# A 64-step recurrence: z stored into the accumulating PSUM bank by identity products

## Chip, cores and metric

The kernel runs on one core of one Trainium2 chip. The metric is the device time of one execution in microseconds, the median of several runs. All data are fp32.

## What is computed

The reference is an audio tower of four layers over 64 sequences of 246 tokens and 128 features. The change touches one stage of it, the recurrence inside the third layer's attention ("L2_attn", 8 heads of 64 features). In the form in which the kernel computes it, for every token position, head and step t of 64:

```
e_t    = exp(h_{t-1} - max h_{t-1});  r_t = 1 / sum(e_t)        (64 features)
w_s    = r_t * (K_s . e_t)                       for the n = t + 1 steps s <= t
h_t    = z_t + sum over s <= t of w_s * U_s      (64 features, stored as result hs)
```

e_0 is all ones and r_0 is 1/64. K, U and z (`kr`, `ur`, `zz`) come from the stage before. So the work of a step grows with t, and h_t is needed before step t + 1 of the same chain can start.

## The kernel before

`recur_stage` (from L2494) holds the whole recurrence. Two dynamic loops run over 4 pairs of heads and 2 halves of the token positions: 8 passes. Within a pass 123 positions are cut into two groups `a` of 62 and 61 positions; with 2 heads each, a group fills 124 or 122 partitions. All 64 steps are written out by hand, and the two groups alternate, so that one works on VectorE while the other is on TensorE. K, U, z of a pass are loaded in 4 chunks of 16 steps on SP's queue (`s_in`), and `Hh` holds z and is overwritten step by step with h.

For one group and one step (n = t + 1), in the order of the dependences:

- VectorE, `dots`: K times e into `pr` (L2608, n x 64 elements), reciprocal of the sum (L2610), sum over features into `dot` (L2613), scale and parity mask into `w` (L2615, `s_dot`).
- TensorE turns w (L2587): a transpose of 124 partitions by 2n columns into `wT` (`s_tr`).
- ScalarE, `spread` (L2563): copies wT into the block-diagonal weights `W` (`s_dg`).
- TensorE (L2596): 62 or 61 products, one a position, of 2n rows by 32 columns with 64 moving columns, four at a time in four column groups, added up in one PSUM bank `acc[a]` (`s_sum`). A product for one position contributes zeros to the other rows of its 32, which is why 16 of them share a column group.
- VectorE, `finish`: adds z, h = acc + z into `Hh` (L2621), then the negated maximum (L2622, `s_mx`).
- ScalarE, `exped` (L2569): e = exp(h + mx) with the sum as accumulator output, which shows as a second row, ACTIVATION_READ_ACCUMULATOR (`s_ex`).

Each engine takes its instructions in program order. VectorE: dots(0,t), finish(1,t-1), dots(1,t), finish(0,t). ScalarE: spread(0,t), exped(1,t-1), spread(1,t), exped(0,t). TensorE: turn(0,t), products(0,t), turn(1,t), products(1,t). SP stores a chunk of `Hh` once both groups' maxima of its last step are done (L2552 to L2555).

Of the kernel before, what the change touches and what calls it, by code (L numbers as in the profile page):

```python
# [8 lines left out]
ALU = mybir.AluOpType  # L9
# [432 lines left out]
SC = 8  # L442
# [1688 lines left out]
FD = 64  # L2131
# [362 lines left out]
def recur_stage(nc, c, kr, ur, zz, hs):  # L2494
# [8 lines left out]
    with Stage(nc, "recur") as st:  # L2503
# [10 lines left out]
        rs = [st.sb(f"rs{a}", [CP, 1]) for a in range(2)]  # L2514
        ri = [st.sb(f"ri{a}", [CP, 1]) for a in range(2)]
        wT = [st.ps(f"wT{a}", [128, 512]) for a in range(2)]
        acc = [st.ps(f"acc{a}", [128, 512]) for a in range(2)]
        s_in = [st.sem(f"loaded{k}") for k in range(NL)]
        s_own = [st.sem(f"own{a}") for a in range(2)]
        s_dot = [st.sem(f"dots{a}") for a in range(2)]  # L2520
# [2 lines left out]
        s_sum = [st.sem(f"summed{a}") for a in range(2)]  # L2523
        s_mx = [st.sem(f"max{a}") for a in range(2)]
        s_ex = [st.sem(f"exp{a}") for a in range(2)]
        s_out = st.sem("stored")
        V = nc.vector

# [8 lines left out]
        with nc.Fori(0, FH // 2) as i, nc.Fori(0, 2) as half, st.step() as block:  # L2537
            @block.sync
            def _(sp):
                chains = lambda t, a: t[i, bass.ds(half * HT + GROUPS[a][0], GROUPS[a][1])].rearrange("t h s d -> (t h) s d")  # L2540
                for k in range(NL):
                    r = slice(k * SC, (k + 1) * SC)
                    for a, (t0, tg) in enumerate(GROUPS):
                        for p in (slice(0, 112), slice(112, 2 * tg)):
                            sp.dma_start(K[a][p, r, :], chains(kr, a)[p, r, :]).then_inc(s_in[k], 16)
                            sp.dma_start(Hh[a][p, r, :], chains(zz, a)[p, r, :]).then_inc(s_in[k], 16)
                        sp.dma_start(U[a][2 * SC * k:2 * SC * (k + 1), 0:tg, :],
                                     ur[i].rearrange("s h t d -> (s h) t d")[2 * SC * k:2 * SC * (k + 1), bass.ds(half * HT + t0, tg), :]).then_inc(s_in[k], 16)
                for k in range(NL):
                    r = slice(k * SC, (k + 1) * SC)  # L2550
                    for a, (t0, tg) in enumerate(GROUPS):
                        sp.wait_ge(s_mx[a], (k + 1) * SC)  # L2552
                        for p in (slice(0, 112), slice(112, 2 * tg)):
                            sp.dma_start(hs[i].rearrange("s t h d -> (t h) s d")[bass.ds(half * (2 * HT) + 2 * t0 + p.start, p.stop - p.start), r, :],
                                         Hh[a][p, r, :]).then_inc(s_out, 16)  # L2555
                sp.wait_ge(s_out, 64 * NL)

            @block.scalar
            def _(act):
                def spread(a, t):  # L2560
                    n, tg = t + 1, GROUPS[a][1]
                    act.wait_ge(s_tr[a], n)
                    nc.scalar.activation(W[a][0:2 * n, 0:34 * TG].rearrange("p (m x) -> p m x", x=34)[:, 0:tg, 0:2],  # L2563
                                         wT[a][0:2 * n, 0:2 * tg].rearrange("p (m h) -> p m h", h=2), ACT.Copy).then_inc(s_dg[a], 1)

                def exped(a, t):
                    cp = 2 * GROUPS[a][1]
                    act.wait_ge(s_mx[a], t + 1)
                    nc.scalar.activation(e[a][0:cp], Hh[a][0:cp, t, :], ACT.Exp, bias=mx[a][0:cp, 0:1],  # L2569
                                         accum_out=rs[a][0:cp, 0:1]).then_inc(s_ex[a], 1)  # L2570

                for t in range(SL):
                    spread(0, t)
                    if t:
                        exped(1, t - 1)
                    spread(1, t)
                    if t + 1 < SL:
                        exped(0, t)

            @block.tensor  # L2580
            def _(pe):
                for t in range(SL):
                    n = t + 1
                    for a, (t0, tg) in enumerate(GROUPS):
                        cp = 2 * tg
                        pe.wait_ge(s_dot[a], n)
                        nc.tensor.transpose(wT[a][0:2 * n, 0:cp], w[a][0:cp, 0:n, :].rearrange("p s h -> p (s h)"),  # L2587
                                            c.ident[0:cp, 0:cp]).then_inc(s_tr[a], 1)
                        if t % SC == 0:
                            pe.wait_ge(s_in[t // SC], 160)  # L2590
                        pe.wait_ge(s_dg[a], n)
                        for j in range(16):
                            for q in range(4):
                                m = 16 * q + j
                                if m < tg:
                                    ins = nc.tensor.matmul(acc[a][32 * q:32 * q + 32, 0:FD], W[a][0:2 * n, WQ * q + 32 * j:WQ * q + 32 * j + 32],  # L2596
                                                           U[a][0:2 * n, m, :], start=(j == 0), stop=(j == 15 or m + 1 == tg))
                        ins.then_inc(s_sum[a], 1)

            @block.vector  # L2600
            def _(dve):
# [16 lines left out]
                def finish(a, t):  # L2618
                    cp = 2 * GROUPS[a][1]
                    dve.wait_ge(s_sum[a], t + 1)  # L2620
                    own[a](V.tensor_tensor(Hh[a][0:cp, t, :], acc[a][0:cp, 0:FD], Hh[a][0:cp, t, :], ALU.add))  # L2621
                    V.tensor_reduce(mx[a][0:cp], Hh[a][0:cp, t, :], AX.X, ALU.max, negate=True).then_inc(s_mx[a], 1)  # L2622

                for a in range(2):
                    own[a](V.memset(e[a][:], 1.0))
# [1129 lines left out]
```

## Time and profile before

| | us |
|---|---|
| median of 3 runs | 25499.4 |
| lowest, highest | 25471.2, 25502.3 |
| profiled execution | 25494.0 |
| its span | 25492.3 |
| of the span, recurrence (8 passes) | about 13960 to 21110 |

Over the whole span TensorE's products are busy 15738.5 us (62%), VectorE 12959.8 (51%), ScalarE 5715.3 (22%), GpSimd 2368.2 (9%). A line of the span in 40 slices shows where each engine works, as a digit for tenths of its time; the recurrence is slices 22 to 33:

```profile
PE   3423577745457787787787665565466554455776
DVE  6512455551153343343343777877877782213555
ACT  0001244411023333333333100000010001123442
PEclk9566566657679999999998555555555556676776
```

PE is TensorE's products and PEld its weight loads, which overlap them; DVE is VectorE, ACT ScalarE. PEclk is the clock that TensorE was granted, in tenths of 2.4 GHz.

### The profile page before, as it was taken

What the parts mean: (1) busy time and instruction counts of PE and PEld (TensorE: products, weight loads), DVE (VectorE), ACT (ScalarE), POOL (GpSimd) and SP (SyncE); (2) the same over time, 40 slices, a digit from 0 to 9 for tenths busy, and PEclk for the clock granted to TensorE, in tenths of its full rate; (3) what the DMA queues carried; (4) which work ended last, traced back from release to release, by engine and by line L of the source; (5) the groups of instructions that cost most, each with busy time, mean ns of one, the idle gap of its engine ahead of it and who ended that gap; (6) DMA issues with size and microseconds to landing.
All of it is one profiled execution on the core that took longest, in us unless ns stands there. A gap on an engine that the chain in (4) does not pass through costs nothing. (4 is left out here: it accounts for less than half of the span.)

```text
span 25492.3 us, 660904 instructions
## 1 busy us (share of the span) xinstructions
PE 15738.5 (62%) x292639; PEld 13161.1 (52%) x292639; DVE 12959.8 (51%) x23794; ACT 5715.3 (22%) x12048; POOL 2368.2 (9%) x1280
## 2 busy tenths in 40 slices
PE   3423577745457787787787665565466554455776
PEld 2412566633246666666666554555455444344554
DVE  6512455551153343343343777877877782213555
ACT  0001244411023333333333100000010001123442
POOL 0063000013501011011010000000000000010001
PEclk9566566657679999999998555555555556676776
DMA  0222100022221101101101011011101104004663
GB/s 17 80 38 59 36 14 14 14 62 60 36 61 17 18 17 17 18 17 17 18 17 29 14 26 24 7 26 26 22 12 26 25 6 139 19 20 146 187 182 89
DMA packets 1549770, 1066.76 MB, mean 42 GB/s; under 512 B 819722, under 2 KB 1473965, under 8 KB 1528109
## 3 DMA queue, kind: packets, MB, share of 16 engines
q1 hardware_dynamic: 1319715, 967.03, 15.3%
q0 software_dynamic: 227328, 57.19, 1.5%
q8 instruction: 2466, 40.40, 0.7%
q14 instruction: 261, 2.14, 0.0%
HBM read 537.19 MB, written 484.53 MB: 40 GB/s over the span
## 5 line engine op out<-in xcount | busy, mean ns | idle before, releaser
L2596 PE MATMUL recur_acc<-recur_U,recur_W 2*32 2x64 f32 (+7 forms) x125952 | 3713.9, 311 | 552.9 <-ACT recur_W L2563 385.1
L2596 PEld LDWEIGHTS recur_acc<-recur_U,recur_W 2*32 2x32 f32 (+7 forms) x125952 | 3467.5, 172 | 850.7 <-ACT recur_W L2563 629.3
L2608 DVE TENSOR_TENSOR recur_pr<-recur_K,recur_e 124x64 f32<-124x64 f32 (+60 forms) x1024 | 2381.1, 2325 | 817.7 <-ACT recur_e L2569 694.9
L2276 PE MATMUL delta_pS<-delta_B 64*64 64x64 f32 x55104 | 2287.4, 234 | 792.4 <-issue 783.5
L2276 PEld LDWEIGHTS delta_pS<-delta_B 64*64 64x64 f32 x55104 | 2035.2, 145 | 1338.1 <-issue 1333.5
L2395 DVE TENSOR_TENSOR delta_U<-delta_U,delta_pR 128x256 f32<-128x256 f32 x1968 | 828.6, 421 | 3386.8 <-PE delta_pR L2276 3379.4
L2613 DVE TENSOR_REDUCE recur_dot<-recur_pr 124x1 f32<-124x64 f32 (+60 forms) x1024 | 2375.8, 2320 | 35.4
L2350 ACT ACTIVATE delta_B<-delta_pS 128x512 f32<-128x512 f32 (+1 forms) x1968 | 1067.7, 543 | 4449.7 <-PE delta_pS L2276 4449.7
L2587 PE MATMUL recur_wT<-const_ident,recur_w 124*2 124x124 f32 (+60 forms) x1024 | 424.5, 415 | 2457.6 <-DVE recur_w L2615 2455.6
L2276 PE MATMUL delta_pR<-delta_U,delta_B 64*64 64x64 f32 x39360 | 1725.6, 224 | 303.0 <-DVE delta_Z L2404 192.4
L2563 ACT ACTIVATE recur_W<-recur_wT 2x124 f32<-2x124 f32 (+60 forms) x1024 | 287.1, 280 | 6504.2 <-PE recur_wT L2587 6504.2
L2276 PEld LDWEIGHTS delta_pR<-delta_U,delta_B 64*64 64x64 f32 x39360 | 1510.9, 140 | 333.2 <-issue 206.1
L2587 PEld LDWEIGHTS recur_wT<-const_ident,recur_w 124*2 124x2 f32 (+60 forms) x1024 | 133.4, 130 | 2677.7 <-DVE recur_w L2615 2634.1
L2381 POOL TENSOR_TENSOR delta_QK<-delta_QK,delta_mx 128x1536 f32<-128x1536 f32 x123 | 339.4, 2760 | 5306.1 <-DVE delta_mx L2409 5306.1
L2276 PE MATMUL delta_gp<-delta_W,delta_xc 128*128 128x16 f32 x1476 | 767.9, 603 | 33.5 <-DVE delta_xc L2389 33.5
L2276 PE MATMUL delta_pR<-delta_P,delta_B 64*64 64x64 f32 x15744 | 674.8, 221 | 90.6 <-DVE delta_P L2401 73.1
L1206 PE MATMUL experts_tp<-const_ident,experts_xg 123*128 123x123 f32 x256 | 49.5, 328 | 1093.8 <-DMA experts_xg<-xp,experts_ij 1093.8
L2823 POOL IOTA choice_ios<- 123x64 f32 x1 | 0.2, 185 | 7715.6 <-POOLq L78 7715.6
L2276 PEld LDWEIGHTS delta_pR<-delta_P,delta_B 64*64 64x64 f32 x15744 | 585.9, 134 | 145.9 <-issue 117.4
L1167 POOL DMA_INDIRECT hB<-experts_y,experts_ij x256 | 616.5, 2408 | 370.8 <-DVE experts_y L1185 200.2
L2276 PE MATMUL delta_gp<-delta_KT 64*64 64x64 f32 x11808 | 531.7, 223 | 159.9 <-ACT delta_KT L2369 98.4
L1206 PEld LDWEIGHTS experts_tp<-const_ident,experts_xg 123*128 123x128 f32 x256 | 37.1, 172 | 1122.4 <-DMA experts_xg<-xp,experts_ij 1104.9
(574 smaller groups left out, 27572.6 us busy)
## 6 DMA issues: line engine op xcount, KB each, us to landing
scr<-rel_BD SPq DMA_DIRECT2D x128, 1288.0 KB
rel_sc<-scr SPq DMA_DIRECT2D x128, 861.0 KB
xnT<-ln_xT SPq DMA_DIRECT2D x64, 492.0 KB, 3.0
kr<-delta_QK SPq DMA_DIRECT2D x492, 64.0 KB
ur<-delta_Uf SPq DMA_DIRECT2D x492, 64.0 KB
zz<-delta_Z SPq DMA_DIRECT2D x492, 64.0 KB
recur_K<-kr SPq DMA_DIRECT2D x64, 448.0 KB
recur_H<-zz SPq DMA_DIRECT2D x64, 448.0 KB
```

What stands on the lines that cost most here:

```text
L1167: nc.gpsimd.indirect_dma_start(acc[:, :], bass.IndirectOffsetOnAxis(ap=ij[:, k, t:t + 1], axis=0), y[:, k, t, :], None, compute_op=ALU.add ...
L1206: nc.tensor.transpose(tp[:, t, 0:HT], xg[:, k, t, 0:D], c.ident[0:HT, 0:HT]).then_inc(s_tp, 1)
L2276: return nc.tensor.matmul(o, l, r, start=True, stop=True)
L2350: nc.scalar.activation(later(k, l + 1)[0][:, :, 0:m, :], pS[k][:, :, 0:m, :], ACT.Copy).then_inc(s_ac[k], 1)
L2381: nc.gpsimd.tensor_tensor(qk, qk, wide_of(mx), ALU.subtract).then_inc(s_sh, 1)
L2395: V.tensor_tensor(later(k, l + 1)[1][:], u[:], pR[k][l % 2][:, 0:4, :], ALU.subtract if l == 0 else ALU.add).then_inc(s_dv[k], 1)
L2563: nc.scalar.activation(W[a][0:2 * n, 0:34 * TG].rearrange("p (m x) -> p m x", x=34)[:, 0:tg, 0:2], wT[a][0:2 * n, 0:2 * tg].rearrange("p ( ...
L2587: nc.tensor.transpose(wT[a][0:2 * n, 0:cp], w[a][0:cp, 0:n, :].rearrange("p s h -> p (s h)"), c.ident[0:cp, 0:cp]).then_inc(s_tr[a], 1)
L2596: ins = nc.tensor.matmul(acc[a][32 * q:32 * q + 32, 0:FD], W[a][0:2 * n, WQ * q + 32 * j:WQ * q + 32 * j + 32], U[a][0:2 * n, m, :], start ...
L2608: V.tensor_tensor(pr[a][0:cp, 0:n, :], K[a][0:cp, 0:n, :], e[a][0:cp, None, :].to_broadcast([cp, n, FD]), ALU.mult).then_inc(s_own[a], 1)
L2613: own[a](V.tensor_reduce(dot[a][0:cp, 0:n], pr[a][0:cp, 0:n, :], AX.X, ALU.add))
L2823: nc.gpsimd.iota(ios[:], pattern=[[1, CS]], base=0, channel_multiplier=0, allow_small_or_imprecise_dtypes=True).then_inc(s_po, 1)
```

## The change

z_t is no longer added by VectorE. Ahead of a step's turn TensorE multiplies z_t, as it lies in `Hh`, by the four 32-column slices of the identity matrix (`start=True`), so the PSUM bank begins with z_t, and all the other products add to it (`start=False`). The maximum and the exponential read the bank in PSUM. ScalarE copies the bank into `Hh` behind the exponential (`keep`, a new semaphore `s_cp`). Each group has two banks, used by even and odd steps; the identity products of step t wait for the copy of step t - 2. SP's stores wait for the copy where they waited for the maximum. TensorE's wait for the loads moves ahead of the turn.

```diff
-        acc = [st.ps(f"acc{a}", [128, 512]) for a in range(2)]
+        acc = [[st.ps(f"acc{a}{q}", [128, 512]) for q in range(2)] for a in range(2)]
...
+        s_cp = [st.sem(f"kept{a}") for a in range(2)]
...
-                        sp.wait_ge(s_mx[a], (k + 1) * SC)
+                        sp.wait_ge(s_cp[a], (k + 1) * SC)
...
-                    nc.scalar.activation(e[a][0:cp], Hh[a][0:cp, t, :], ACT.Exp, bias=mx[a][0:cp, 0:1],
+                    nc.scalar.activation(e[a][0:cp], acc[a][t % 2][0:cp, 0:FD], ACT.Exp, bias=mx[a][0:cp, 0:1],
                                          accum_out=rs[a][0:cp, 0:1]).then_inc(s_ex[a], 1)
+
+                def keep(a, t):
+                    cp = 2 * GROUPS[a][1]
+                    act.wait_ge(s_mx[a], t + 1)
+                    nc.scalar.activation(Hh[a][0:cp, t, :], acc[a][t % 2][0:cp, 0:FD], ACT.Copy).then_inc(s_cp[a], 1)
 
                 for t in range(SL):
                     spread(0, t)
                     if t:
                         exped(1, t - 1)
+                        keep(1, t - 1)
                     spread(1, t)
                     if t + 1 < SL:
                         exped(0, t)
+                    keep(0, t)
+                keep(1, SL - 1)
...
+                        if t % SC == 0:
+                            pe.wait_ge(s_in[t // SC], 160)
+                        if t >= 2:
+                            pe.wait_ge(s_cp[a], t - 1)
+                        for q in range(4):
+                            nc.tensor.matmul(acc[a][t % 2][32 * q:32 * q + 32, 0:FD], c.ident[0:cp, 32 * q:32 * q + 32], Hh[a][0:cp, t, :],
+                                             start=True, stop=False)
                         pe.wait_ge(s_dot[a], n)
                         nc.tensor.transpose(wT[a][0:2 * n, 0:cp], w[a][0:cp, 0:n, :].rearrange("p s h -> p (s h)"),
                                             c.ident[0:cp, 0:cp]).then_inc(s_tr[a], 1)
-                        if t % SC == 0:
-                            pe.wait_ge(s_in[t // SC], 160)
                         pe.wait_ge(s_dg[a], n)
                         for j in range(16):
                             for q in range(4):
                                 m = 16 * q + j
                                 if m < tg:
-                                    ins = nc.tensor.matmul(acc[a][32 * q:32 * q + 32, 0:FD], W[a][0:2 * n, WQ * q + 32 * j:WQ * q + 32 * j + 32],
-                                                           U[a][0:2 * n, m, :], start=(j == 0), stop=(j == 15 or m + 1 == tg))
+                                    ins = nc.tensor.matmul(acc[a][t % 2][32 * q:32 * q + 32, 0:FD], W[a][0:2 * n, WQ * q + 32 * j:WQ * q + 32 * j + 32],
+                                                           U[a][0:2 * n, m, :], start=False, stop=(j == 15 or m + 1 == tg))
...
-                    own[a](V.tensor_tensor(Hh[a][0:cp, t, :], acc[a][0:cp, 0:FD], Hh[a][0:cp, t, :], ALU.add))
-                    V.tensor_reduce(mx[a][0:cp], Hh[a][0:cp, t, :], AX.X, ALU.max, negate=True).then_inc(s_mx[a], 1)
+                    V.tensor_reduce(mx[a][0:cp], acc[a][t % 2][0:cp, 0:FD], AX.X, ALU.max, negate=True).then_inc(s_mx[a], 1)
```

## Rows read from the trace of the kernel before

**Rows 1.** The page's groups: count, busy us, mean ns, idle before

```profile
L2596 PE MATMUL recur_acc<-recur_U,recur_W 2*32 2x64 f32 (+7 forms) x125952 | 3713.9, 311 | 552.9 <-ACT recur_W L2563 385.1
L2608 DVE TENSOR_TENSOR recur_pr<-recur_K,recur_e 124x64 f32<-124x64 f32 (+60 forms) x1024 | 2381.1, 2325 | 817.7 <-ACT recur_e L2569 694.9
```

**Rows 2.** Windows (length, PE, PEld, DVE, ACT, POOL busy, clock, DMA), and one burst

```profile
14060.00:14150.00 90.00, 82.33 (x2601) 72.77 (x2597) 50.97 (x123) 14.01 (x63) 0.00 (x0) 0.50 0.02 4
...
14700.00:14850.00 150.00, 60.84 (x1859) 53.11 (x1853) 136.49 (x91) 8.99 (x45) 0.00 (x0) 0.61 0.01 2
...
14652.44 3.33 PE L2596 MATMUL recur_acc<-recur_U,recur_W 108*32 108x64 f32 x124 [0.38 <-ACT recur_W L2563]
```

**Rows 3.** Timeline (start, us, engine, line) of a half-step at n = 10

```profile
14104.70 0.09 PEld L2587 LDWEIGHTS recur_wT<-const_ident,recur_w 122*20 122x20 f32 x1 [0.17 <-issue]
14104.71 0.37 PE L2587 MATMUL recur_wT<-const_ident,recur_w 122*20 122x122 f32 x1
...
14105.09 0.22 DVE L2622 TENSOR_REDUCE recur_mx<-recur_H 124x1 f32<-124x64 f32 x1
14105.12 0.28 ACT L2563 ACTIVATE recur_W<-recur_wT 20x122 f32<-20x122 f32 x1 [3.64 <-PE recur_wT L2587]
14105.35 0.35 ACT L2569 ACTIVATE recur_e<-recur_H,recur_mx 124x64 f32<-124x64 f32 x1
...
14105.45 3.63 PE L2596 MATMUL recur_acc<-recur_U,recur_W 20*32 20x64 f32 x122 [0.36 <-ACT recur_W L2563]
```

**Rows 4.** Timeline of TensorE: turns that end n = 3, 16, 21, and the next

```profile
14044.55 0.37 PE L2587 MATMUL recur_wT<-const_ident,recur_w 122*6 122x122 f32 x1
...
14156.39 0.39 PE L2587 MATMUL recur_wT<-const_ident,recur_w 122*32 122x122 f32 x1
...
14200.93 0.39 PE L2587 MATMUL recur_wT<-const_ident,recur_w 122*42 122x122 f32 x1 [0.24 <-DVE recur_w L2615]
...
14205.69 0.40 PE L2587 MATMUL recur_wT<-const_ident,recur_w 124*44 124x124 f32 x1 [0.38 <-DVE recur_w L2615]
```

**Rows 5.** Timeline of a half-step at n = 62

```profile
14806.54 0.35 DVE L2615 SCALAR_TENSOR_TENSOR recur_w<-recur_dot,recur_ri,recur_par 124x124 f32<-124x124 f32 x1
14806.81 0.22 DVE L2621 TENSOR_TENSOR recur_H<-recur_acc,recur_H 122x64 f32<-122x64 f32 x1
...
14806.94 0.47 PE L2587 MATMUL recur_wT<-const_ident,recur_w 124*124 124x124 f32 x1 [5.78 <-DVE recur_w L2615]
14807.06 0.22 DVE L2622 TENSOR_REDUCE recur_mx<-recur_H 122x1 f32<-122x64 f32 x1
14807.45 0.29 ACT L2563 ACTIVATE recur_W<-recur_wT 124x124 f32<-124x124 f32 x1 [9.66 <-PE recur_wT L2587]
14807.62 0.34 ACT L2569 ACTIVATE recur_e<-recur_H,recur_mx 122x64 f32<-122x64 f32 x1
...
14808.08 4.29 DVE L2608 TENSOR_TENSOR recur_pr<-recur_K,recur_e 122x3968 f32<-122x3968 f32 x1 [0.80 <-ACT recur_e L2569]
```

**Rows 6.** Timeline of weight loads, last stage, then the stage behind the recurrence

```profile
25303.31 0.49 PEld L3654 LDWEIGHTS last_p<-last_ws,last_xa 128*123 128x123 f32 x2 [0.23 <-issue]
25304.03 0.48 PEld L3653 LDWEIGHTS last_p<-last_be,last_hx 16*123 16x123 f32 x2 [0.23 <-issue]
...
21140.88 0.95 PEld L2708 LDWEIGHTS dout_yp<-dout_wo,dout_tT 128*123 128x123 f32 x8
21141.75 0.46 PEld L2699 LDWEIGHTS dout_tp<-const_ident,dout_t 123*128 123x128 f32 x4
```

**Rows 7.** ScalarE's groups by form: count, busy us, mean ns, idle before

```profile
L2569 ACT ACTIVATE recur_e<-recur_H,recur_mx 124x64 f32<-124x64 f32 x504 | 171.1, 340 | 0.0
L1483 ACT ACTIVATE liquid_a<-liquid_pp,liquid_cols 128x64 f32<-128x64 f32 x246 | 77.2, 314 | 227.8 <-PE liquid_pp L1475 227.8
...
L2362 ACT ACTIVATE delta_sb<-delta_sb 128x16 f32<-128x16 f32 x123 | 26.5, 216 | 1.4
L2357 ACT ACTIVATE delta_sb<-delta_gp 128x16 f32<-128x16 f32 x123 | 22.5, 183 | 1.4
```

## The prediction

> **What bounds the kernel now.** I read the groups of instructions of the recurrence first, then its windows, then the timeline of one half-step from each part. A half-step is one group `a` at one step `t`; n = t + 1 is the number of stored steps that the dot products run over. There are 64 steps, 2 groups and 8 passes of the outer loops, so 1024 half-steps, 128 a pass. The busiest two groups [rows 1] are the products into `acc` on TensorE (L2596: 125952 rows for 1024 half-steps, 123 each, so a group's 62 or 61 fp32 products show as 124 or 122 rows) and the multiply of K by e on VectorE (L2608), whose mean hides that it grows with n.
>
> The windows [rows 2] show two parts. At 14060 to 14150 us TensorE is busy 82.33 us of 90 and VectorE 50.97: TensorE bounds it. At 14700 to 14850 VectorE is busy 136.49 us of 150 and TensorE 60.84: VectorE, or a chain through it, bounds it. ScalarE is busy 14.01 and 8.99 us, so it is never the bound by itself.
>
> In the first part a half-step is a ring on TensorE alone [rows 3]: the turn of w (L2587) starts at 14104.71, ScalarE spreads it at 14105.12, the products run 3.63 us from 14105.45, and the next turn follows. VectorE's maximum (14105.09) and the exponential (14105.35) lie under the products. From the last turn of n = 3 (14044.55) to the last of n = 16 (14156.39) are 26 half-steps [rows 4], 4.30 us each; to the last of n = 21 (14200.93) are 10 more, 44.54 us, already partly set by VectorE; the next takes 4.76.
>
> In the second part [rows 5] the ring is: w ready on VectorE (starts 14806.54), turn 14806.94, spread 14807.45, exponential of the *other* group 14807.62, VectorE's next multiply 14808.08. VectorE does the add (14806.81) and the maximum (14807.06 to 14807.28) beside the turn. The reader is to see what the exponential waits for: the maximum is done 0.34 us before it starts, while the spread started 0.17 us before it, and L2563 stands ahead of L2569 in ScalarE's queue. The add is not on this ring.
>
> **The add that goes.** It lasts 0.22 us and holds the maximum back by 0.25 (14806.81 to 14807.06) [rows 5]. In the second part nothing is gained: the maximum would be ready 0.59 us instead of 0.34 before an exponential that still queues behind the spread. VectorE just idles longer before L2608. In the first part the products are the cover: the exponential could move from 0.23 to 0.17 us behind the spread [rows 3, 5], under a burst of 3.63. So: 0. If that cover were gone it would be worth 0.25 a half-step (a rival below). The maximum reads PSUM instead of SBUF; the add read PSUM in the same 0.22 us, so I take no change, and it has 0.34 us of slack.
>
> **The exponential reads PSUM.** From SBUF with a bias column it takes 340 ns at 64 elements; the activation of another stage, 64 elements from PSUM with a bias column, takes 314; two 16-element ones take 216 from SBUF and 183 from PSUM [rows 7]. So 26 to 33 ns less, if it reaches the ring. I take 25 ns, bounds 0 and 35. It counts where the exponential is on the ring: n = 22 to 64, 43 x 2 x 8 = 688 half-steps: -17 us (bounds 0 and -24).
>
> **The identity products.** Four a half-step, fp32, 124 rows by 32 columns, so 8 more matmul rows. By the burst's own rate (3.63 us / 124 = 29.3 ns) [rows 3] they take 0.234 us. They stand before the turn in TensorE's queue. Where TensorE idles before the turn (5.78 us at n = 62 [rows 5]) they are free. Where it does not, all of it is on the ring, and so is a second thing: TensorE's pipeline empties when the size of tile changes. The turn's weight load in the first part starts after 0.17 us in which the loader waits for nothing shown [rows 3]; in the last stage, where 16-row and 128-row products alternate, it is 0.23 [rows 6]; where transposes and products of the same size alternate (L2699, L2708) there is none [rows 6]. The Trainium skill, TensorEngine Tiling (Array Packing), Key Properties, says that changing the tiling mode drains TensorE; these rows agree.
>
> For n up to 16 the burst has up to 32 rows, the identity products 124 by 32, the turn 124 by 2n, up to 32 columns. The emptying moves ahead of the identity products, and none is added behind them if the turn's tile is as small as its columns. Cost 0.24; lower bound 0.12 (one of two rounds of four hidden in the switch), upper 0.234 + 0.17 = 0.40. For n = 17 to 32 the turn has 34 to 64 columns, another size, so the emptying comes twice; I take 0.37, near the upper bound, since part of the 0.17 overlaps.
>
> Sum per pass: n = 4 to 16, 26 x 0.24 = 6.24. For n = 1 to 3, 6 x 0.24 = 1.44. For n = 17 to 21, ten half-steps of 4.31 + 0.37 = 4.68 are 46.8 in place of 44.54 [rows 4]: 2.26. From n = 22 the half-step (4.76) is longer than that and covers it. Together 9.94, x 8 = 79.5 us. With both lower bounds (0.12; 0.234 over n = 17 to 21, where only the shorter of the half-steps grow, about 1.1): 4.9 x 8 = 39. With 0.40 everywhere: (12.8 + 2.6) x 8 = 123.
>
> **Added waits.** TensorE waits on `s_cp` of step t - 2, with the turn and the products queued behind it: that copy was done a whole step earlier. Its wait on the loads moves ahead of the turn, but the turn needed dot products of the same loads. ScalarE's copy `keep` (about 0.28 us like L2563 [rows 3]) follows its exponential directly, and the next spread behind it comes over 3 us later. SP's stores wait for the copy in place of the maximum: at the end of a pass 0.25 goes and about 0.28 comes, 0. Two banks a group mean no reader is waited for.
>
> **The sum.** The profiled execution took 25494.0 us (span 25492.3), 5.4 below the median of 25499.4. 25494.0 + 79.5 - 17.2 = 25556. Bounds of the unknown costs together: 25494 + 39 - 24 = 25509 and 25494 + 123 = 25617. About 0.2% (51 us) is what a measurement of this kernel can tell from no change.
>
> **Rivals.**
> A, the forecast: 25556, chance 0.64.
> B, faster: the add does sit on the second part's ring, because the exponential's start is set by the maximum and not by the spread. For: the wait before L2608 is put down to the exponential, which needs the maximum. Against: the 0.34 us of slack [rows 5]. It decides if the exponential starts less than 0.17 us behind the spread once the maximum is early. Then 688 x 0.25 = 172 us go: 25384. Chance 0.08.
> C, nothing to be seen: the identity products slip into the time in which TensorE changes tile size, and the exponential gives its full 35 ns: 25490 to 25515. Against: a burst's products follow each other at 29.3 ns a row with no slack between them, so eight more rows should take their share. Chance 0.09.
> D, dearer: the turn is always of full width, so the emptying is paid twice at every n: 0.13 more on 32 half-steps x 8 = 33 us: 25589. For: the turn shows one row where an fp32 product shows two, so it runs in a mode of its own. Against: nothing in the trace separates it. Chance 0.16.
> The Trainium skill, the same page, Gotcha 2, says that column tiling excludes the transpose mode with fp32, which is rival D; no row here shows it.
> E, the clock: TensorE's granted clock is 0.50 (1.2 GHz) through the first part although it is busy 92% [rows 2], and 0.61 on average in the second, where the products have over 100 rows. If 124-row products lifted it in the first part, bursts would shorten: one that lay partly at 2.4 GHz took 3.33 us against 3.63 [rows 2, 3]. At 0.5 us for a whole burst, 32 x 8 x 0.5 = 128 us go: 25428. Against: 8 of 132 rows are few. Chance 0.03.
> The Trainium skill, TensorE: Matmul & The Clock Gate, Part 1, says that activity releases a clock that is halved by default; the 92% at 0.50 speaks against reading that by busy time alone.
>
> **How the numbers follow.** The forecast is the likeliest case's, 25556. Its own spread (25509 to 25617) straddles 25499 + 51 = 25550: of A's 0.64 I give 0.36 to slower and 0.28 to the same; D is slower (0.16), C the same (0.09), B and E faster (0.11). That is faster 0.11, same 0.37, slower 0.52. The range 25490 to 25617 leaves out B, E and a little of the rest.
>
> **What would show it.** Turn to turn at n = 4 to 16: 4.54 us, two-fold emptying 4.67, hidden 4.3. At n = 17 to 21: 4.68. At n = 62: 10.26 less 0.025, B 10.0. The exponential still 0.17 us behind the spread and the idle time before L2608 up from 0.80 to about 1.0. The exponential at 310 ns. What would make it wrong: another order on ScalarE's ring than I read, or the read of PSUM by two engines slowing one of them.

## Result and profile after

The changed kernel takes 25566.69 us in the median of 8 runs (25541.24 to 25592.09), the kernel before 25485.58 in 8 runs beside it (25471.23 to 25502.32). The ratio is 1.0031, with a 95% interval of 1.0020 to 1.0042: slower by about 0.3%. The forecast was 25556, and the time lies in its range (25490 to 25617). The profiled execution took 25571.98 us, 77.9 more than that of before.

The table counts from turn to turn of w on TensorE, all 8 passes added up, after less before; each number is a sum over the turns' starts in the two traces. A half-step counts to the step whose turn ends it.

| stretch | half-steps a pass | one before | one after | all, us | forecast, us |
|---|---|---|---|---|---|
| n = 1 to 3 | 6 | loads decide | | +6.1 | +11.5 |
| n = 4 to 16 | 26 | 4.30 | 4.67 | +77.5 | +49.9 |
| n = 17 to 21 | 10 | 4.31 to 4.64 | 4.69 to 4.70 | +19.3 | +18.1 |
| n = 22 to 64 | 86 | 10.26 at n = 62 | 10.23 | -23.9 | -17.2 |
| sum | 128 | | | +79.0 | +62.3 |

Between the passes and ahead of the first turn another -0.7 comes, which makes +78.3 at the last turn: the whole difference lies in the recurrence.

The half-step at n = 10 of after, which answers to [rows 3]. The view is the timeline: start, us, engine, line, operation, and in brackets the idle time before with what ended it.

```profile
14105.68 0.20 PEld L2600 LDWEIGHTS recur_acc<-recur_H,const_ident 122*32 122x32 f32 x8 [0.17 <-issue]
14105.68 0.44 PE L2600 MATMUL recur_acc<-recur_H,const_ident 122*32 122x64 f32 x8
...
14106.05 0.09 PEld L2603 LDWEIGHTS recur_wT<-const_ident,recur_w 122*20 122x20 f32 x1 [0.17 <-issue]
14106.05 0.38 PE L2603 MATMUL recur_wT<-const_ident,recur_w 122*20 122x122 f32 x1
14106.46 0.28 ACT L2564 ACTIVATE recur_W<-recur_wT 20x122 f32<-20x122 f32 x1 [4.01 <-PE recur_wT L2603]
14106.63 0.29 ACT L2570 ACTIVATE recur_e<-recur_acc,recur_mx 124x64 f32<-124x64 f32 x1
14106.79 3.39 PEld L2610 LDWEIGHTS recur_acc<-recur_U,recur_W 20*32 20x32 f32 x122 [0.65 <-ACT recur_W L2564]
14106.79 3.63 PE L2610 MATMUL recur_acc<-recur_U,recur_W 20*32 20x64 f32 x122 [0.36 <-ACT recur_W L2564]
...
14110.35 0.20 PEld L2600 LDWEIGHTS recur_acc<-recur_H,const_ident 124*32 124x32 f32 x8 [0.17 <-issue]
...
14110.72 0.38 PE L2603 MATMUL recur_wT<-const_ident,recur_w 124*22 124x124 f32 x1
```

The ring reads off the starts. Identity products to turn: 14105.68 to 14106.05, 0.37. Turn to burst: 0.74, as before [rows 3]. Burst to the next identity products: 3.56, just what it was from burst to turn (4.30 - 0.74). So the whole growth is the 0.37 between the start of the identity products and the turn, and in it stands the second 0.17 in which the weight loader waits for nothing shown. Before, there was one such gap; now there is one ahead of L2600 and one ahead of L2603.

The half-step at n = 62 of after, which answers to [rows 5], again from the timeline:

```profile
14811.97 0.35 DVE L2629 SCALAR_TENSOR_TENSOR recur_w<-recur_dot,recur_ri,recur_par 124x124 f32<-124x124 f32 x1
14812.23 0.22 DVE L2635 TENSOR_REDUCE recur_mx<-recur_acc 122x1 f32<-122x64 f32 x1
...
14812.87 0.29 ACT L2564 ACTIVATE recur_W<-recur_wT 124x124 f32<-124x124 f32 x1 [9.55 <-PE recur_wT L2603]
14813.04 0.31 ACT L2570 ACTIVATE recur_e<-recur_acc,recur_mx 122x64 f32<-122x64 f32 x1
...
14813.47 4.29 DVE L2622 TENSOR_TENSOR recur_pr<-recur_K,recur_e 122x3968 f32<-122x3968 f32 x1 [1.02 <-ACT recur_e L2570]
```

The add is gone and the maximum starts 0.25 us sooner, but the exponential still starts 0.17 behind the spread. The maximum is done at 14812.45, 0.59 before the exponential. VectorE's idle time before the next multiply is 1.02 instead of 0.80: what the add gave back is waited away, less the 0.03 by which the exponential is shorter.

Four groups of after over the recurrence (count, busy us, mean ns, idle before and what ended it), beside [rows 1]:

```profile
L2622 DVE TENSOR_TENSOR recur_pr<-recur_K,recur_e 124x64 f32<-124x64 f32 (+60 forms) x1024 | 2380.8, 2325 | 1133.4 <-ACT recur_e L2570 1008.1 <-DMA recur_U<-ur 125.3
L2600 PE MATMUL recur_acc<-recur_H,const_ident 124*32 124x64 f32 (+1 forms) x8192 | 532.7, 309 | 224.1 <-DMA recur_U<-ur 224.1
L2570 ACT ACTIVATE recur_e<-recur_acc,recur_mx 124x64 f32<-124x64 f32 x1008 | 301.4, 299 | 0.0
L2576 ACT ACTIVATE recur_H<-recur_acc 124x64 f32<-124x64 f32 (+1 forms) x1024 | 215.8, 211 | 30.6 <-DVE recur_mx L2635 30.6
```

VectorE waits 1133.4 us before its multiply instead of 817.7; the identity products are 8192 rows, 8 a half-step; the exponential takes 299 ns on average.

### The profile page after: what moved, and what is told of

Read it like the earlier page. It is cut to its first block and busy times, and to the rows that moved or that the text cites. A ratio compares the mean times of both kernels' runs of the same rounds, so it can differ in the third digit from the quotient of the medians.

```text
span 25570.0 us, 677290 instructions
## 1 busy us (share of the span) xinstructions
PE 16032.1 (63%) x300831; PEld 13367.6 (52%) x300831; DVE 12724.3 (50%) x22770; ACT 5774.8 (23%) x13072; POOL 2371.8 (9%) x1280
## 5 line engine op out<-in xcount | busy, mean ns | idle before, releaser
L2622 DVE TENSOR_TENSOR recur_pr<-recur_K,recur_e 124x64 f32<-124x64 f32 (+60 forms) x1024 | 2380.8, 2325 | 1133.4 <-ACT recur_e L2570 1008.1
L2603 PE MATMUL recur_wT<-const_ident,recur_w 124*2 124x124 f32 (+60 forms) x1024 | 424.5, 415 | 2034.6 <-DVE recur_w L2629 2033.0
L2603 PEld LDWEIGHTS recur_wT<-const_ident,recur_w 124*2 124x2 f32 (+60 forms) x1024 | 133.6, 130 | 2251.0 <-DVE recur_w L2629 2197.8
L2600 PE MATMUL recur_acc<-recur_H,const_ident 124*32 124x64 f32 (+1 forms) x8192 | 532.7, 309 | 224.1 <-DMA recur_U<-ur 224.1
```

Source lines behind the costliest of these rows:

```text
L2600: nc.tensor.matmul(acc[a][t % 2][32 * q:32 * q + 32, 0:FD], c.ident[0:cp, 32 * q:32 * q + 32], Hh[a][0:cp, t, :], start=True, stop=False)
L2622: V.tensor_tensor(pr[a][0:cp, 0:n, :], K[a][0:cp, 0:n, :], e[a][0:cp, None, :].to_broadcast([cp, n, FD]), ALU.mult).then_inc(s_own[a], 1)
```

## First set of experiments: which part costs, which gives

The theory is that of the prediction with one term grown: identity products ahead of the turn cost their time and a second emptying at every n up to 21; the add is worth nothing; the exponential's read of PSUM gives 0.035 a half-step from n = 22. The rival is that other parts carry the difference: the waits added on TensorE, the copy on ScalarE, or PSUM being read by two engines. All four kernels of this set are compared with the same runs of before, median 25509.9 us.

**Products alone.** The kernel before, with four products of K's rows by the identity slices into a bank that nobody reads.

```diff
+        spare = [st.ps(f"spare{a}", [128, 512]) for a in range(2)]
...
+                        if t % SC == 0:
+                            pe.wait_ge(s_in[t // SC], 160)
+                        for q in range(4):
+                            nc.tensor.matmul(spare[a][32 * q:32 * q + 32, 0:FD], c.ident[0:cp, 32 * q:32 * q + 32], K[a][0:cp, t, :],
+                                             start=True, stop=True)
                         pe.wait_ge(s_dot[a], n)
...
-                        if t % SC == 0:
-                            pe.wait_ge(s_in[t // SC], 160)
                         pe.wait_ge(s_dg[a], n)
```

> The kernel before, with four fp32 identity products (of K's rows, 124 by 32, 64 moving columns) added ahead of each turn into a spare PSUM bank that nobody reads. Nothing else of the change. Theory (the products and a second emptying of TensorE lie on TensorE's ring up to n = 21 and nowhere else): turn to turn 4.67 us at n = 4 to 16 against 4.30, 4.69 at n = 17 to 21, and exactly the old 10.26 at n = 62, so about +97 us over n = 4 to 21 and +100 in all, 20 to 25 us more than the whole change costs. Rival (the loss comes from two engines reading the accumulating bank, or from ScalarE's copy): this kernel costs under 20 us.

Measured 25616.76 us, ratio 1.0044 (1.0028 to 1.0059). Turn to turn at n = 4 to 16 it is 4.67, +77.5 us in all; n = 17 to 21 gives +19.2, n = 1 to 3 +5.3, n = 22 to 64 -0.1. These are after's own losses, with no add removed, no new wait on a copy, and no read moved. TensorE's wait for the loads stands ahead of the turn here too, as in the change. The timeline of this kernel at n = 8 has both gaps:

```profile
14108.76 0.20 PEld L2590 LDWEIGHTS recur_spare<-recur_K,const_ident 122*32 122x32 f32 x8 [0.17 <-issue]
...
14109.13 0.09 PEld L2593 LDWEIGHTS recur_wT<-const_ident,recur_w 122*16 122x16 f32 x1 [0.17 <-issue]
```

**No add.** The kernel before without the add of z; the maximum reads the bank in PSUM.

```diff
-                    own[a](V.tensor_tensor(Hh[a][0:cp, t, :], acc[a][0:cp, 0:FD], Hh[a][0:cp, t, :], ALU.add))
-                    V.tensor_reduce(mx[a][0:cp], Hh[a][0:cp, t, :], AX.X, ALU.max, negate=True).then_inc(s_mx[a], 1)
+                    V.tensor_reduce(mx[a][0:cp], acc[a][0:cp, 0:FD], AX.X, ALU.max, negate=True).then_inc(s_mx[a], 1)
```

> The kernel before with VectorE's add of z left out and the maximum taken from PSUM, so the result lacks z. Theory (the exponential waits behind the spread in ScalarE's queue, not for the maximum): turn to turn unchanged within 0.01 us at n = 62 and at n = 10, VectorE's idle time before its multiply up by 0.2 to 0.25, total within 10 us of before. Rival B (the add lies on the second part's ring): 0.25 us less a half-step from n = 22 on, 172 us less in all.

Measured 25502.61 us, ratio 0.9997 (0.9988 to 1.0006): no change. n = 4 to 16 gives 0.0 us, n = 17 to 21 +1.1, n = 22 to 64 +0.1. 1024 instructions of 0.22 us are gone from VectorE and nothing comes of it: VectorE's idle time before its multiply rises from 817.7 [rows 1] to 1055.5 us, about as much as the adds had taken. Rival B of the prediction falls with this run. The group over the recurrence:

```profile
L2608 DVE TENSOR_TENSOR recur_pr<-recur_K,recur_e 124x64 f32<-124x64 f32 (+60 forms) x1024 | 2381.2, 2325 | 1055.5 <-ACT recur_e L2569 930.5 <-DMA recur_U<-ur 124.9
```

**Exponential from PSUM.** The kernel before, with the exponential alone moved to the bank.

```diff
-                    nc.scalar.activation(e[a][0:cp], Hh[a][0:cp, t, :], ACT.Exp, bias=mx[a][0:cp, 0:1],
+                    nc.scalar.activation(e[a][0:cp], acc[a][0:cp, 0:FD], ACT.Exp, bias=mx[a][0:cp, 0:1],
```

> The kernel before with the add kept, the exponential reading the accumulating PSUM bank (so e lacks z) in place of the sum in SBUF. Theory: the exponential's row falls from 340 to 300 to 310 ns, turn to turn falls by 0.03 to 0.04 us from n = 22 on and by nothing at n = 4 to 16, 24 us less in all. Rival (the 0.035 us a late half-step come from the add that is gone, or from VectorE's read of PSUM): no change.

Measured 25482.47 us, ratio 0.9990 (0.9981 to 1.0000). n = 22 to 64 gives -23.5 us, beside after's -23.9, and n = 4 to 16 +0.1. So the exponential's read alone gives the whole gain of the second part. Its group over the recurrence:

```profile
L2569 ACT ACTIVATE recur_e<-recur_acc,recur_mx 124x64 f32<-124x64 f32 x1008 | 308.3, 306 | 0.0
```

306 ns against 339 in before's group over the same stretch (340 for one of its forms [rows 7]), and 688 half-steps by 0.034 is 23.5 us.

**Behind the turn.** The kernel after, with the identity products and the waits ahead of them moved behind the turn in TensorE's queue. All else of the change stays, the copy and its wait too.

```diff
-                        if t % SC == 0:
-                            pe.wait_ge(s_in[t // SC], 160)
-                        if t >= 2:
-                            pe.wait_ge(s_cp[a], t - 1)
-                        for q in range(4):
-                            nc.tensor.matmul(acc[a][t % 2][32 * q:32 * q + 32, 0:FD], c.ident[0:cp, 32 * q:32 * q + 32], Hh[a][0:cp, t, :],
-                                             start=True, stop=False)
                         pe.wait_ge(s_dot[a], n)
                         nc.tensor.transpose(wT[a][0:2 * n, 0:cp], w[a][0:cp, 0:n, :].rearrange("p s h -> p (s h)"),
                                             c.ident[0:cp, 0:cp]).then_inc(s_tr[a], 1)
+                        if t % SC == 0:
+                            pe.wait_ge(s_in[t // SC], 160)
+                        if t >= 2:
+                            pe.wait_ge(s_cp[a], t - 1)
+                        for q in range(4):
+                            nc.tensor.matmul(acc[a][t % 2][32 * q:32 * q + 32, 0:FD], c.ident[0:cp, 32 * q:32 * q + 32], Hh[a][0:cp, t, :],
+                                             start=True, stop=False)
                         pe.wait_ge(s_dg[a], n)
```

> The changed kernel with its four identity products (and their two waits) issued behind the turn instead of ahead of it, so that they run while ScalarE spreads the turned weights. Theory: the products find the 0.36 us in which TensorE waits for the spread; their last row starts about 0.44 us after the turn's load and the burst's load about 0.74 after, so turn to turn goes back to 4.30 to 4.35 at n = 4 to 16, the late half-steps keep their gain of 0.035, and the total is 20 to 25 us under the kernel before (up to 15 over it if the burst's start slips by 0.15 us). Rival (the eight rows cost their time wherever they stand, as TensorE is 92% busy): 0.23 us or more a half-step up to n = 21, 50 to 60 us over before less 24.

Measured 25483.54 us, ratio 0.9989 (0.9980 to 0.9998). n = 4 to 16 gives +1.7 us, all of it in one of the eight passes, n = 17 to 21 -4.0, n = 22 to 64 -23.6. The half-step at n = 10 of this kernel, from the timeline:

```profile
14101.85 0.38 PE L2596 MATMUL recur_wT<-const_ident,recur_w 124*20 124x124 f32 x1
...
14102.16 0.20 PEld L2603 LDWEIGHTS recur_acc<-recur_H,const_ident 124*32 124x32 f32 x8 [0.22 <-issue]
14102.16 0.44 PE L2603 MATMUL recur_acc<-recur_H,const_ident 124*32 124x64 f32 x8
14102.26 0.28 ACT L2564 ACTIVATE recur_W<-recur_wT 20x124 f32<-20x124 f32 x1 [3.65 <-PE recur_wT L2596]
...
14102.59 3.39 PEld L2610 LDWEIGHTS recur_acc<-recur_U,recur_W 20*32 20x32 f32 x124 [0.23 <-ACT recur_W L2564]
14102.59 3.63 PE L2610 MATMUL recur_acc<-recur_U,recur_W 20*32 20x64 f32 x124
```

The products run from 14102.16 to 14102.60, while ScalarE spreads the turned w for the burst, and the burst starts 0.74 after the turn, as it does in after and before. The idle time of the loader before the burst fell from 0.65 to 0.23: it holds the products and their emptying now. So the same work, one instruction further down the queue, costs nothing that shows in the half-steps. Nor do the copy, its semaphore and the second bank: they are all in this kernel.

The parts add up: +96.6 (products alone) and -25.0 (exponential) for n from 4 on is +71.6, and after has +72.9. The stretch n = 1 to 3, where the loads decide, scatters: the kernel without the add has -3.4 there and that with the moved exponential -6.2, though neither does less TensorE work. So after's +6.1 there can't be put down to the change with certainty.

## Second set: what hides the add, and what the second gap is

The median of before beside these is 25510.7 us.

The prediction put the add's worth at 0.25 a half-step if its cover were gone, and named the cover: the exponential queues behind the spread. If the exponential stands first in ScalarE's queue, its start is set by the maximum, and then the add counts. The rival is that VectorE's own work sets the ring and the order doesn't matter.

**Exponential first, kernel before.** From t = 20 on ScalarE's order is exped(1, t-1), spread(0, t), exped(0, t), spread(1, t).

```diff
                 for t in range(SL):
+                    first = t >= 20
+                    if first:
+                        exped(1, t - 1)
                     spread(0, t)
-                    if t:
+                    if t and not first:
                         exped(1, t - 1)
+                    if first and t + 1 < SL:
+                        exped(0, t)
                     spread(1, t)
-                    if t + 1 < SL:
+                    if not first and t + 1 < SL:
                         exped(0, t)
```

> The kernel before with one thing changed: from step 20 on (n = 21) ScalarE's queue holds each exponential ahead of the other group's spread instead of behind it. Theory (the exponential is held by the spread in front of it, by 0.30 us once the maximum is there): it now starts 0.04 us after the maximum ends, and turn to turn falls by 0.30 us at n = 62 (10.26 to 9.96); between n = 21 and 24 TensorE's ring, which now has the exponential ahead of its spread, sets about 4.7 us. In all 195 to 200 us less. Rival (the order of ScalarE's queue is nothing, the second part is bound by VectorE's own work): no change at n = 62.

Measured 25338.87 us, ratio 0.9938 (0.9921 to 0.9955). At n = 62 a half-step is 9.965 instead of 10.26, and n = 22 to 64 gives -166.4 us. That is less than the 195 to 200 us expected, for two reasons: the gain grows with n and reaches the expected 0.30 nowhere (-0.23 at n = 26, -0.29 at n = 62), and at n = 22 the half-step got longer, 4.77 to 4.87.

The first reason lies in the turn. Before, the chain from w to the next multiply runs through turn and spread; now it runs through add and maximum. From the start of the turn to that of the spread it is 0.44 us at n = 26 and 0.50 at n = 62 in before (means of 16 half-steps); the turn itself lasts 0.39 with 42 columns [rows 4] and 0.47 with 124 [rows 5]. That stretch is no longer on the ring, so its growth of 0.06 is gained on top. From the start of w's instruction to the multiply it is 1.53 us in before at n = 62 and 1.24 here, and 1.40 and 1.17 at n = 26.

The second reason shows in the timeline at n = 22 of this kernel:

```profile
14211.22 0.23 DVE L2626 TENSOR_TENSOR recur_H<-recur_acc,recur_H 122x64 f32<-122x64 f32 x1 [0.22 <-PE recur_acc L2601]
14211.48 0.22 DVE L2627 TENSOR_REDUCE recur_mx<-recur_H 122x1 f32<-122x64 f32 x1
14211.73 0.35 ACT L2569 ACTIVATE recur_e<-recur_H,recur_mx 122x64 f32<-122x64 f32 x1 [4.26 <-DVE recur_mx L2627]
...
14212.08 0.26 ACT L2563 ACTIVATE recur_W<-recur_wT 44x124 f32<-44x124 f32 x1
...
14212.40 3.63 PE L2601 MATMUL recur_acc<-recur_U,recur_W 44*32 44x64 f32 x124 [0.91 <-ACT recur_W L2563]
```

While TensorE is near its bound, the add waits for the end of a burst (0.22 <-PE) and the next burst waits, through the spread, for add, maximum and exponential. From add to burst is 1.18 us; before, the spread waited for the turn alone, and turn to burst was 0.77 at this n. A new ring has taken the place of the old one: burst, add, maximum, exponential, spread, burst. Only where VectorE sets the pace does the new order shorten the step: at n = 23 it is even, from n = 24 on it gains.

**Exponential first, products behind the turn.** The kernel of the run "behind the turn" with the same order of ScalarE; the copy stays behind the spread. Against that kernel:

```diff
                 for t in range(SL):
+                    first = t >= 20
+                    if first:
+                        exped(1, t - 1)
                     spread(0, t)
-                    if t:
+                    if t and not first:
                         exped(1, t - 1)
+                    if t:
                         keep(1, t - 1)
+                    if first and t + 1 < SL:
+                        exped(0, t)
                     spread(1, t)
-                    if t + 1 < SL:
+                    if not first and t + 1 < SL:
                         exped(0, t)
                     keep(0, t)
```

> The changed kernel with the identity products behind the turn and, from step 20 on, each exponential ahead of the spread, the copy into H behind the spread. Against the run with only the order changed this tells what the add is worth once nothing else covers it. Theory: the maximum is ready 0.25 us earlier than there, the exponential reads PSUM in 0.035 us less, so turn to turn at n = 62 falls by another 0.28 to 0.29, to 9.67 (0.59 under the kernel before); TensorE's ring sets about 4.65 us from n = 21 to 25. In all 380 to 395 us less than before. Rival (the add is covered by something else too, the turn for one): 9.93 at n = 62 and 220 us less.

Measured 25146.16 us, ratio 0.9860 (0.9843 to 0.9876), 1.4% under the kernel before, and so under the changed kernel too. n = 62 is 9.675, as expected; n = 22 to 64 gives -366.3 us, n = 17 to 21 -6.1, n = 4 to 16 -0.1. The median is about 365 us under before's, less than the 380 to 395 expected: the smaller gain at small n, found in the run before, is in this kernel too. From the timeline at n = 58 of this kernel:

```profile
14707.17 0.22 DVE L2641 TENSOR_REDUCE recur_mx<-recur_acc 124x1 f32<-124x64 f32 x1
...
14707.42 0.31 ACT L2570 ACTIVATE recur_e<-recur_acc,recur_mx 124x64 f32<-124x64 f32 x1 [8.36 <-DVE recur_mx L2641]
...
14707.80 0.29 ACT L2564 ACTIVATE recur_W<-recur_wT 116x122 f32<-116x122 f32 x1
14707.85 4.09 DVE L2628 TENSOR_TENSOR recur_pr<-recur_K,recur_e 124x3776 f32<-124x3776 f32 x1 [0.47 <-ACT recur_e L2570]
```

The exponential now waits for the maximum (8.36 <-DVE recur_mx) and no longer queues behind the spread. VectorE's idle time before the multiply is 0.47, where it was 0.80 [rows 5] and in after 1.02. In the group over the recurrence it is 658.3 us instead of after's 1133.4:

```profile
L2628 DVE TENSOR_TENSOR recur_pr<-recur_K,recur_e 124x64 f32<-124x64 f32 (+60 forms) x1024 | 2381.1, 2325 | 658.3 <-ACT recur_e L2570 534.5 <-DMA recur_U<-ur 123.8
```

The run before it, with the same order of ScalarE's queue and the add still in place, shows what stood between w and the maximum (its timeline at n = 57):

```profile
14705.52 0.34 DVE L2620 SCALAR_TENSOR_TENSOR recur_w<-recur_dot,recur_ri,recur_par 122x114 f32<-122x114 f32 x1
14705.78 0.22 DVE L2626 TENSOR_TENSOR recur_H<-recur_acc,recur_H 124x64 f32<-124x64 f32 x1
14706.03 0.22 DVE L2627 TENSOR_REDUCE recur_mx<-recur_H 124x1 f32<-124x64 f32 x1
14706.28 0.35 ACT L2569 ACTIVATE recur_e<-recur_H,recur_mx 124x64 f32<-124x64 f32 x1 [8.68 <-DVE recur_mx L2627]
```

Against that run, the half-step at n = 62 is 0.29 shorter. No kernel has only the new order and no add, but the two traces split the difference: from the start of w's instruction to the end of the maximum it is 0.74 us there and 0.48 here, which is the add's 0.25, and from the exponential to the multiply 0.47 there and 0.44 here, which is the read of PSUM (means of 16 half-steps at n = 62). So the same edit, the add's removal, is worth 0 in one order of ScalarE's queue and 0.25 us a half-step in the other. The add's removal also shortens the ring that hurt at n = 22: 4.57 instead of 4.87.

The second gap: is it because the turn has another tile than its columns suggest? Two kernels change one side of the step each. Each has one run, so its time is given without an interval, and the argument rests on its half-steps.

**One wide product.** The kernel after, with one identity product of 124 by 128 in place of four of 124 by 32. If the turn runs at full width whatever its columns, the gap ahead of it goes.

```diff
-                        for q in range(4):
-                            nc.tensor.matmul(acc[a][t % 2][32 * q:32 * q + 32, 0:FD], c.ident[0:cp, 32 * q:32 * q + 32], Hh[a][0:cp, t, :],
-                                             start=True, stop=False)
+                        nc.tensor.matmul(acc[a][t % 2][:, 0:FD], c.ident[0:cp, :], Hh[a][0:cp, t, :], start=True, stop=False)
```

> The changed kernel with one identity product of 124 rows by 128 columns (two matmul rows) in place of four of 32 columns (eight), ahead of the turn as in the change. It asks where the second emptying at n up to 16 comes from. If the turn, a transpose, always runs in a tile of full width (rival D of the prediction), this product has the turn's size, the weight loader does not idle 0.17 us between them, and turn to turn is 4.3 plus two rows of a full load, 0.2 to 0.3 us: 4.50 to 4.60. If the turn's tile is as narrow as its columns and something else empties the pipeline, the idle 0.17 stays and turn to turn is 4.65 to 4.75.

Measured 25630.3 us in its one run. At n = 8, with a turn of 16 columns, from the timeline:

```profile
14105.24 0.50 PEld L2599 LDWEIGHTS recur_acc<-recur_H,const_ident 124*128 124x128 f32 x2 [0.17 <-issue]
14105.24 0.69 PE L2599 MATMUL recur_acc<-recur_H,const_ident 124*128 124x64 f32 x2
...
14105.51 0.24 PEld L2601 LDWEIGHTS recur_wT<-const_ident,recur_w 124*16 124x16 f32 x1
14105.72 0.41 PE L2601 MATMUL recur_wT<-const_ident,recur_w 124*16 124x124 f32 x1
```

The turn's weight load follows with no idle time: the gap is gone, and not only here but at every n from 2 to 21, whether the turn has 4 columns or 42. The time was missed all the same: turn to turn is 4.81 to 4.82, not less than 4.67. The two rows of the wide product load for 0.50 us where the eight narrow ones load for 0.20, so product to turn is 0.48 and turn to burst 0.78, against 0.37 and 0.74: 0.15 more, which is the difference. The expectation had put the wide product at 0.2 to 0.3 us in all; it costs 0.52 (4.82 - 4.30).

**Turn as a product.** The kernel after, where up to n = 16 the turn is an ordinary product with the identity instead of a transpose; its tile is then 124 by at most 32, as that of the identity products.

```diff
-                        nc.tensor.transpose(wT[a][0:2 * n, 0:cp], w[a][0:cp, 0:n, :].rearrange("p s h -> p (s h)"),
-                                            c.ident[0:cp, 0:cp]).then_inc(s_tr[a], 1)
+                        if n <= 16:
+                            nc.tensor.matmul(wT[a][0:2 * n, 0:cp], w[a][0:cp, 0:n, :].rearrange("p s h -> p (s h)"),
+                                             c.ident[0:cp, 0:cp], start=True, stop=True).then_inc(s_tr[a], 1)
+                        else:
+                            nc.tensor.transpose(wT[a][0:2 * n, 0:cp], w[a][0:cp, 0:n, :].rearrange("p s h -> p (s h)"),
+                                                c.ident[0:cp, 0:cp]).then_inc(s_tr[a], 1)
```

> The changed kernel with the turn of n up to 16 done as an ordinary fp32 product with the identity instead of a transpose. Both it and the identity products ahead of it then have 124 rows and up to 32 columns and the same mode. If the second emptying comes from the transpose mode (or from the full width that it is given), the weight loader's 0.17 us of idle time ahead of the turn goes; the product itself shows two rows and streams 122 columns twice, about 0.2 us more, so turn to turn is 4.70 to 4.80 with no idle time ahead of the turn, and n = 17 and up is as in the changed kernel. If the emptying has another cause, the idle time of 0.17 stays and turn to turn is 4.85 to 4.95.

Measured 25619.11 us in its one run. At n = 9, from the timeline:

```profile
14106.20 0.20 PEld L2600 LDWEIGHTS recur_acc<-recur_H,const_ident 122*32 122x32 f32 x8 [0.17 <-issue]
...
14106.31 0.26 PEld L2604 LDWEIGHTS recur_wT<-const_ident,recur_w 122*18 122x18 f32 x2
...
14106.41 0.61 PE L2604 MATMUL recur_wT<-const_ident,recur_w 122*18 122x122 f32 x2
...
14107.39 3.63 PE L2614 MATMUL recur_acc<-recur_U,recur_W 18*32 18x64 f32 x122 [0.36 <-ACT recur_W L2564]
```

No gap again, now with the tile made equal from the other side. Identity products to turn is 0.21 instead of 0.37; turn to burst is 0.98 instead of 0.74, since the fp32 product is two rows of 0.61 in all where the transpose is one of 0.38. 4.67 - 0.16 + 0.24 = 4.75, and 4.75 to 4.76 is measured. This run splits the cost of the change: of 0.37 a half-step, 0.21 is the identity products, and 0.16 is the second emptying.

From n = 17 on this kernel has the transpose again, and with it the idle time of 0.17.

Both runs together say that a transpose counts as another size of tile than a product of the same columns, and the same as a product of full width. The gaps show that; that it is TensorE's pipeline that empties in them is the prediction's reading and fits, but no trace looks inside. The Trainium skill, TensorEngine Tiling (Array Packing), Gotcha 2, says that column tiling excludes the transpose mode with fp32 input: by that rule the narrow turn was never a narrow tile, and these two traces agree. Its price is 0.16 us a half-step here.

## Why the prediction was right, and where it was off

- **Add: 0.** Right, for the reason given. The run without the add gives 0.9997, and the exponential stays 0.17 behind the spread. The run with the other order gives the price of 0.25 once the cover is gone.
- **Exponential: 25 ns, bounds 0 and 35.** The mechanism was right, and the size was off: 0.034 to 0.035 a half-step, -23.9 us instead of -17.2. The nearest rows [rows 7] spanned 26 to 33, and I stayed below them; the instruction took 0.31 instead of 0.34 at n = 62. Those rows were also weaker than I made them: each pair compares two different functions (tanh with the exponential, sigmoid with the square root), and none but the exponential has an accumulator.
- **The maximum's read of PSUM: 0.** Right: 220 ns on average from SBUF in before and from PSUM in after.
- **Identity products, n = 4 to 16: 0.24.** This is the step that failed: 0.373, so +77.5 us instead of +49.9. I had taken that the turn's tile is as small as its columns and that no second gap comes. The second gap came at every n, as in rival D, to which I gave 0.16 beside the forecast's 0.64, and whose estimate of 0.13 more a half-step is what was measured (0.373 - 0.24). The products' own time was near: 0.21 against 0.234. "Nothing in the trace separates it", I wrote; but the transposes and products in [rows 6] that alternate without a gap were all of full width, and the turn with few columns was never seen beside a product of as many rows and columns. What spoke most for D was that the transpose shows as one row where a product shows as two, and I weighed it too low.
- **n = 17 to 21: 4.68.** 4.69 to 4.70. The number is right, its reason is not: the gap is 0.17 there as at n = 4 to 16, so the turn's 34 to 42 columns are not what brings it.
- **n = 1 to 3: +11.5.** +6.1; the scatter of this stretch is as large, so it tells neither way.
- **Rival C's range.** 25490 to 25515 doesn't follow from its own terms: with the products at 0 to the lower bound of 39 us and the exponential at 24, it is 25470 to 25509. Nothing else hangs on it.
- **Added waits, copy, SP's stores: 0.** Right; the run with the products behind the turn has them all and loses nothing in n = 4 to 21 (-2.3 us).
- **Clock, rival E.** It did not rise. The windows of after, and of the fastest kernel at 14060 to 14150, which answer to [rows 2] (length; PE, PEld, DVE, ACT, POOL busy; granted clock; DMA share; GB/s):

```profile
14060.00:14150.00 90.00, 83.00 (x2550) 71.11 (x2554) 42.96 (x96) 12.88 (x80) 0.00 (x0) 0.50 0.01 4
14700.00:14850.00 150.00, 64.10 (x1979) 56.39 (x1979) 133.66 (x76) 10.25 (x60) 0.00 (x0) 0.56 0.01 2
```

```profile
14060.00:14150.00 90.00, 90.00 (x2772) 77.03 (x2763) 43.62 (x105) 13.41 (x82) 0.00 (x0) 0.50 0.02 4
```

The errors had opposite signs: 27.6 us too little in the first part, 6.7 too little gain in the second, 5.4 too much at n = 1 to 3. With 1.2 at n = 17 to 21 they leave 16.7 of 79.0. That the median lies only 10.7 above the forecast is in part luck: besides the opposite signs, the forecast started from a single execution of before, 25494.0, and the median of before beside the result is 8.4 lower. Median to median the change costs 81.1 us, 18.8 more than the 62.3 forecast. Rival D's mechanism came true, though its 25589 is further from the result than the forecast's 25556. The range held, since its bound of 0.40 covered a second emptying. The chances had slower in front, and it is slower.

## What to carry to other kernels

Work that is added to a queue costs what it delays, so place it by the wait behind it: the same eight rows a half-step cost 97 us ahead of the turn and nothing to be seen behind it, under another engine's copy. Before an instruction is taken off one engine, look at what its successor queues behind on the *next* engine; here the exponential stood behind a spread that it did not need, and removing the add was worth 0 until that order was turned round, and then 0.25 us a half-step where VectorE sets the pace. A new order has its own ring, so it is put in only from the step on where the other engine has slack, and the half-steps around the switch are read one by one.

## What the runs showed of the hardware

- A transpose of 124 by 4 to 42 columns is separated from the products of 124 by 32 ahead of it by an idle time of the weight loader of 0.17 us (after), and not from a product of 124 by 128 (one wide product). When the products follow the transpose instead, the gap is 0.19 to 0.22 (behind the turn).
- At a granted clock of 0.50, one fp32 product of 124 by 128 loads its weights in 0.50 us and runs 0.69; four of 124 by 32 in separate column groups load in 0.20 and run 0.44.
- ScalarE's exponential of 64 elements with a bias column takes 298 to 306 ns on average from PSUM and 335 to 347 from SBUF, run by run. VectorE's maximum of 64 elements takes 220 from either. The Trainium skill, ScalarE: Activation LUTs, Step-by-step: what each stage is for, says of where a result is written that ScalarE is closer to PSUM. No run here compares that; what these traces show is a shorter read.
- TensorE shows busy for 90.00 of 90.00 us in the last window above, and the granted clock is 0.50, the 1.2 GHz level. The Trainium skill, TensorE: Matmul & The Clock Gate, Part 1, says that activity releases the halved clock; busy time in these rows did not.
- The second window of after has a mean clock of 0.56 where before had 0.61. That is no effect of the change: over n = 52 to 64 the clock varies from 0.56 to 0.62 between the passes of either trace, and its mean over the eight passes is 0.60 in both.
